# Second attention layer in pairs: two heads to a score bank, two to a transposing bank, copies by ScalarE alone

## What is computed

```python
h = norm(x) * (1.0 + scale) + shift
q = rope(h @ Wq.T)                       # 16 heads
c_kv = h @ Wkd.T                         # latent of 128
k, v = rope(c_kv @ Wku.T), c_kv @ Wvu.T  # 4 heads, each used by 4 query heads
scores = q @ k.T / sqrt(32)              # blocked and windowed: -inf outside
attn = softmax(scores)
x = x + (attn @ v) @ Wo.T
```

## Time and profile before

| | |
|---|---|
| median of 3 runs | 2899.52 us (2898.2 to 2907.24) |
| the profiled execution | 2904.38 us, its span 2902.6 us, mean granted clock 0.894 |
| L1 attention, first load to its last output matmul | 1178.6 to about 1646 us of the span |
| its tile loop | 1224 to 1625 us |
| PE / DVE / ACT / POOL busy in the whole span | 2427.1 / 1624.0 / 1213.8 / 908.3 us |

### The profile page before, as it was taken

The page is one execution under the profiler, slowest core; times in us unless marked ns, Lnnn a source line. Parts: engine busy times, 40 slices in busy tenths (PEclk is TensorE's granted clock), DMA queues, the critical chain, the costliest instruction groups (busy, mean ns, idle before and its releaser), DMA issues. The chain is left out here.

```text
span 2902.6 us, 47820 instructions
## 1 busy us (share of the span) xinstructions
PE 2427.1 (84%) x15668; PEld 1962.4 (68%) x15668; DVE 1624.0 (56%) x4635; ACT 1213.8 (42%) x2990; POOL 908.3 (31%) x982
## 2 busy tenths in 40 slices
PE   4878789798589999688888568889689999996786
PEld 2767677677477888466666457777578888885565
DVE  3777766677654443566556466566543333333876
ACT  2565565566331111366656445556431111112443
POOL 0234332233376676223223113223212112110422
PEclk7989889899899999788678679999899999997898
DMA  6000000000200000100000000000101000001000
GB/s 230 1 1 1 9 2 9 1 2 9 88 15 30 15 29 0 71 30 2 2 1 1 31 4 1 1 0 1 46 20 37 30 22 22 0 0 47 1 29 29
DMA packets 15887, 63.16 MB, mean 22 GB/s; under 512 B 2604, under 2 KB 3500, under 8 KB 10692
## 3 DMA queue, kind: packets, MB, share of 16 engines
q1 hardware_dynamic: 15684, 60.65, 5.8%
HBM read 56.42 MB, written 4.23 MB: 21 GB/s over the span
## 5 line engine op out<-in xcount | busy, mean ns | idle before, releaser
L871 ACT ACTIVATE l0a_prob<-l0a_prob,l0a_nmin 128x512 f32<-128x512 f32 x256 | 185.8, 726 | 202.9 <-DVE l0a_nmin L1129 202.5
L1673 POOL TENSOR_TENSOR l2m_hidl<-l2m_hid,l2m_hidh 128x512 fp32r<-128x512 f32 x64 | 100.9, 1577 | 480.2 <-DVE l2m_hidh L1645 480.2
L1293 POOL TENSOR_TENSOR l0a_prob<-l0a_prob,l0a_rinv 128x512 f32<-128x512 f32 x64 | 66.7, 1042 | 517.9 <-DVE l0a_rinv L1136 517.9
L1529 ACT ACTIVATE l2m_gate<-l2m_psG 128x512 f32<-128x512 f32 x64 | 38.3, 598 | 452.0 <-PE l2m_psU L1462 452.0
L1640 DVE TENSOR_TENSOR l2m_hid<-l2m_gate,l2m_psU 128x512 f32<-128x512 f32 x64 | 44.0, 688 | 300.1 <-ACT l2m_gate L1529 300.1
L702 PE MATMUL l0a_psT<-res_ident,l0a_prob 128*128 128x128 f32 x1024 | 166.2, 287 | 12.0 <-ACT l0a_PT L881 11.8
L1129 DVE CUSTOM_DVE_ANT_0 l0a_prob<-l0a_psS,l0a_mask 128x512 f32<-128x512 f32 x256 | 173.3, 688 | 2.6 <-issue 1.6
L1692 POOL TENSOR_TENSOR res_X<-res_X,l0m_share 128x512 f32<-128x512 f32 x128 | 161.8, 1292 | 25.7 <-DVE l0m_share L1629 24.7
L680 PE MATMUL l0a_psS<-l0a_kT,l0a_qT 96*128 96x512 f32 x256 | 127.9, 501 | 43.5 <-DVE l0a_nmin L1129 28.6
L560 PE MATMUL l0a_psA<-l0a_wh,l0a_hTh 128*128 128x128 f32 (+1 forms) x512 | 152.2, 297 | 12.7 <-DVE l0a_wl L1244 5.8
L702 PEld LDWEIGHTS l0a_psT<-res_ident,l0a_prob 128*128 128x128 f32 x1024 | 133.9, 148 | 38.9 <-ACT l0a_PT L881 17.9
(11 more groups left out here) (399 smaller groups left out, 7785.3 us busy)
## 6 DMA issues: line engine op xcount, KB each, us to landing
l2m_stage<-in_l2m_w SPq DMA_DIRECT2D x8, 1536.0 KB, 6.7
l0m_stage<-in_l0m_w SPq DMA_DIRECT2D x8, 1024.0 KB, 4.8
cond_w<-in_wmod SPq DMA_DIRECT2D x6, 1024.0 KB, 7.9
res_X<-in_x SPq DMA_DIRECT2D x4, 1024.0 KB, 13.4
l0a_prob<-in_l0a_w SPq DMA_DIRECT2D x4, 1024.0 KB, 6.6
l1a_wmod<-in_wmod SPq DMA_DIRECT2D x4, 1024.0 KB, 6.0
out<-res_X SPq DMA_DIRECT2D x4, 1024.0 KB, 4.3
l_stage<-in_l_w SPq DMA_DIRECT2D x3, 1024.0 KB, 7.2
```

The costliest lines, as they stand in the source:

```text
L871: act.activation(prob[:, n % NP, 0:w], src[:, 0:w], ACT.Exp, bias=nmin[:, n % NP:n % NP + 1], scale=-1.0, accum_out=ssum[:, n % NP:n % NP ...
L1293: op = pool.tensor_tensor(x, x, r.to_broadcast([P, w]), ALU.mult)
L1673: pool.tensor_tensor(hidl[:, s % 2, m, :], hid[:, m, :], f32(hidh[:, s % 2, m, :]), ALU.subtract).then_inc(hl_done, 1)
```

## The change

In L1 the tiles go in pairs of heads (2p, 2p + 1):

- `s_bank(n)` is n // 2 mod 3 and `s_part` puts the second head at column 256: a bank of psS holds two tiles. AHEAD is 2: an even step n issues the scores of tiles n + 2 and n + 3, an odd step none. The wait is for the minima of the pair before in that bank, five tiles back; `s_done` rises by two after the second matmul.
- the transposes of both heads go in the odd step n, for tiles n - 7 and n - 6, into the two halves of a psT bank; `pT_mm` rises by two at the end. The wait is for the copy two pairs back.
- ACT copies both heads with one ACTIVATE (128 x 512, or 128 x 256 for the first query tile) in the next, even step, ahead of the exponential. DVE copies none.
- `weigh` waits for the copy of the second pair.
- the plan of jobs is as it was.

Beside this, R.sc and R.cT are kept with 4 columns; the padded array c32 is made where it is used: by ACT in the first stage, and by POOL (`padded_rows`: a memset and two copies) at the start of the L0 MLP and of the L1 attention. `pick` is loaded again in each of these two stages, one more DMA on SP ahead of the weights, and their counts on `small_in` rise by one. The instructions of L0 and L2 attention, of the L2 MLP and of the experts are the same.

```diff
+def padded_rows(pool, R, c32, c32_zero, c32_done):
+
+    pool.memset(c32[:], 0.0).then_inc(c32_zero, 1)
+    pool.wait_ge(c32_zero, 1)
+    pool.tensor_copy(c32[:, 0, :, 0:B], R.sc[:])
+    pool.tensor_copy(c32[:, 1, :, 0:B], R.cT[:]).then_inc(c32_done, 1)
...
-    AHEAD = 2 if L is L0 else 1
+    AHEAD = 1 if L is L2 else 2
...
-        NSMALL = 3 if is1 else 2
+        NSMALL = 4 if is1 else 2
...
             n = n % NTILE
+            if is1:
+                return n // 2 % NS
...
-            return next(d for d in range(1, NTILE) if s_bank(n - d) == s_bank(n))
+            return next(d for d in range(1 + is1, NTILE) if s_bank(n - d) == s_bank(n))
+
+        def s_part(n):
+
+            return n % 2 * 256 if is1 else 0
...
+                    sp.dma_start(pick[:], D["pick"]).then_inc(small_in, 16)
...
-                    if n >= since(n) or not first:
+                    if is1 and n % 2 == 1:
+                        pass
+                    elif n >= since(n) or not first:
                         pe.wait_ge(min_done, b * NTILE + (n - since(n) + 1))
...
+                        if n % 2 == 0:
+                            return
...
-                    mm.then_inc(s_done, 1)
+                    mm.then_inc(s_done, 2 if is1 else 1)
 
                 def pT_copied(b, m):
 
+                    if is1:
+                        return pT_act, 2 * U * b + (m // 2 + 1)
...
                 def transposes(b, m, first):
 
-                    if not (first and m < 2):
-                        pe.wait_ge(*pT_copied(b, m - 2))
+                    if is1 and m % 2 == 0:
+                        return
+                    if not (first and m < 2 + 2 * is1):
+                        pe.wait_ge(*pT_copied(b, m - 2 - 2 * is1))
...
+                    for i in ((m - 1, m) if is1 else (m,)):
...
-                        if n + AHEAD < NTILE:
-                            scores(b, n + AHEAD, first)
-                        elif more and n < NTILE:
-                            scores(b + 1, n + AHEAD - NTILE, False)
+                        for k in ((n + AHEAD, n + AHEAD + 1) if is1 and n % 2 == 0 else () if is1 else (n + AHEAD,)):
+                            if k < NTILE:
+                                scores(b, k, first)
+                            elif more and n < NTILE:
+                                scores(b + 1, k - NTILE, False)
...
+                    if is1:
+                        act.activation(PT[:, j - 1:j + 1, 0:w],
+                                       psT[m // 2 % 2].rearrange("p (j w) -> p j w", j=2)[:, :, 0:w],
+                                       ACT.Copy).then_inc(pT_act, 1)
+                        return
...
-                        copy = m is not None and (m - CL) % 4 < 3 and m - CL < NTILE and not (first and m < CL)
+                        copy = m is not None and m - CL < NTILE and not (first and m < CL)
+                        copy = copy and ((m - CL) % 2 == 1 if is1 else (m - CL) % 4 < 3)
...
-                        if m is not None and (m - CL) % 4 == 3 and m - CL < NTILE and not (first and m < CL):
+                        if not is1 and m is not None and (m - CL) % 4 == 3 and m - CL < NTILE and not (first and m < CL):
```

More of the change, by code:

```diff
@@ L106, in bcast_rows, with modulation_products @@
     return bass.AP(ap.tensor, ap.offset, [[0, n]] + list(ap.ap))
-def modulation_products(pe, R, g, w, ps):
-    src = R.sc if g in MOD_COND else R.cT
+def modulation_products(pe, rows, g, w, ps):
+    src = rows[:, 0 if g in MOD_COND else 1]
     for k in range(NK):
@@ L149, in condition @@
         rows = S.sb("rows", [P, 2, C])
+        pick = S.sb("pick", [P, B])
+        c32 = S.sb("c32", [P, 1, NK, COLS])
+        c32_zero = S.sem("c32_zero")
         pm = [S.ps(f"pm{i}", [P, 512]) for i in range(2)]
@@ L189, in _ @@
                 act.wait_ge(small_in, 8 * 16)
-                act.activation(R.sc[:], R.cT[:], ACT.Silu).then_inc(silu_done, 1)
+                act.activation(R.sc[:], R.cT[:], ACT.Silu)
+                act.wait_ge(c32_zero, 1)
+                act.activation(c32[:, 0, :, 0:B], R.cT[:], ACT.Silu).then_inc(silu_done, 1)
                 act.wait_ge(tabs, 1)
@@ L205, in sums @@
                         pe.wait_ge(mod_read, g - 1)
-                    modulation_sums(pe, R, rows[:, g % 2], ps[g % 2]).then_inc(mod_sum, 1)
+                    modulation_sums(pe, pick, rows[:, g % 2], ps[g % 2]).then_inc(mod_sum, 1)
                 pe.wait_ge(silu_done, 1)
@@ L226, in _ @@
             def _(v):
+                v.memset(c32[:], 0.0).then_inc(c32_zero, 1)
                 v.wait_ge(id_done, 1)
@@ L631, in run @@
                         pe.wait_ge(mod_rows, x + 1)
-                        modulation_sums(pe, R, rows, psA[i]).then_inc(mod_sum, 1)
+                        modulation_sums(pe, pick, rows, psA[i]).then_inc(mod_sum, 1)
                         freed[i] = [(mod_done, x + 1)]
@@ L673, in scores @@
                             pe.wait_ge(kT_done, L.nks * (g + 1))
-                    if n >= since(n) or not first:
+                    if is1 and n % 2 == 1:
+                        pass
+                    elif n >= since(n) or not first:
                         pe.wait_ge(min_done, b * NTILE + (n - since(n) + 1))
                     w = L.width[qt]
-                    q, out = qT[:, j, qt * P:(qt + 1) * P], psS[s_bank(n)][:, 0:w]
+                    q, out = qT[:, j, qt * P:(qt + 1) * P], psS[s_bank(n)][:, s_part(n):s_part(n) + w]
                     if is0:
@@ L694, in transposes @@
                 def transposes(b, m, first):
-                    if not (first and m < 2):
-                        pe.wait_ge(*pT_copied(b, m - 2))
+                    if is1 and m % 2 == 0:
+                        return
+                    if not (first and m < 2 + 2 * is1):
+                        pe.wait_ge(*pT_copied(b, m - 2 - 2 * is1))
                     pe.wait_ge(p_done, b * NTILE + (m + 1))
                     qt = m // 4 % NT
-                    for c in range(L.parts[qt]):
-                        k0 = (FAR if qt and c == 0 else 0) if is1 else c * P
-                        mm = pe.transpose(psT[m % 2][:, c * P:(c + 1) * P], prob[:, m % NP, k0:k0 + P], R.ident[:])
-                    mm.then_inc(pT_mm, 1)
+                    for i in ((m - 1, m) if is1 else (m,)):
+                        ps = psT[m // 2 % 2][:, i % 2 * 256:] if is1 else psT[m % 2]
+                        for c in range(L.parts[qt]):
+                            k0 = (FAR if qt and c == 0 else 0) if is1 else c * P
+                            mm = pe.transpose(ps[:, c * P:(c + 1) * P], prob[:, i % NP, k0:k0 + P], R.ident[:])
+                    mm.then_inc(pT_mm, 2 if is1 else 1)
                 def weigh(b, u, first):
                     hg, qt = divmod(u % U, NT)
-                    pe.wait_ge(*pT_copied(b, 4 * u + 2))
+                    if not is1:
+                        pe.wait_ge(*pT_copied(b, 4 * u + 2))
                     pe.wait_ge(*pT_copied(b, 4 * u + 3))
@@ L1128, in minima @@
                     v.memset(beat[:, n % NP:n % NP + 1], 0.0)
-                    v.tensor_tensor_reduce(prob[:, n % NP, 0:w], psS[s_bank(n)][:, 0:w], other,
+                    v.tensor_tensor_reduce(prob[:, n % NP, 0:w], psS[s_bank(n)][:, s_part(n):s_part(n) + w], other,
                                            -L.scale, BIG, ALU.add, ALU.min,
@@ L1476, in sums @@
                         pe.wait_ge(mod_read, n)
-                    modulation_sums(pe, R, rows, psM[1]).then_inc(mod_sum, 1)
+                    modulation_sums(pe, pick, rows, psM[1]).then_inc(mod_sum, 1)
                 body(0, True)
                 if not swiglu:
+                    pe.wait_ge(c32_done, 1)
                     modulation(0, L1_SCALE)
@@ L2072, in layout @@
     a = {k: np.asarray(v) for k, v in i.items()}
-    d = {"x": a["x"], "condT": np.pad(tiles(a["cond_2048"].T), ((0, 0), (0, 0), (0, COLS - B)))}
+    d = {"x": a["x"], "condT": tiles(a["cond_2048"].T)}
     d["pick"] = np.tile(np.eye(COLS, B, dtype=np.float32), (NK, 1))
```

35 lines of the change are left out of this document (23 added, 12 removed).

## The result

The changed kernel took 2952.35 us in the median of 4 runs (2951.14 to 2959.52), the kernel before 2899.7 us. The ratio is 1.0171, with a 95% interval of 1.0149 to 1.0193: 52.6 us slower, where the forecast was 22.4 us slower and the range ended at 2947.

A forecast was written before the change was run, and what follows sets the result against it. No engine was taken to fill L1's tile loop: PE, DVE and ACT are late in turn, PE waiting 41.4 us. Terms -10 + 1.5 + 0 + 21.6 + 4.8 + 3.6 + 0.9 = +22.4 on 2899.5 gave 2922 us, range 2882 to 2947.

The forecast's parts named there:

- the step it rested on: L1 group boundaries: paired scores, issued sooner, make PE wait for ACT's qT copies; +21.6, +4.8 and +3.6 us.
- the price of a boundary: L1 waits for qT: 2.4 us at nine ordinary boundaries, +4.8 at three with output projections, +3.6 at three with the latent.
- the ring of psT: L1 transposes wait two pairs back, but `weigh` waits for ACT's later copy: +1.5 us for three units, 0 elsewhere.
- The copies: L1 loop: DVE loses 63 copies, 24.5 us of work, counting where DVE sets the pace: -10 us, between 0 and -24.5.
- Pairs on prob and psS: L1 loop: even tiles' minima need transposes one step later, psS has five tiles of slack: 0, between -3 and +3 us.
- Starts: Stage starts in L1 attention and the MLP: one more DMA on SP delays small loads and weights, +0.9 us.
- Rival 2: L1 loop: pausing once a unit, PE stays at 1.2 GHz, 0.8 us a unit, about 2946 us; chance 0.12.
- Rivals 1 and 3: 1: half of the 41.4 us recovered, boundaries free, about 2880 us, chance 0.21. 3: gains and waits cancel, 2900, 0.15.
- Outside L1: L0 and L2 attention, whose loops are unchanged, should keep their times.

The follow-up runs named there:

- q_early: Changed kernel with the next head group's q and k transposes two and one steps earlier, so ACT's qT copies come two steps earlier: L1 attention 482.68 us, ratio 1.0087.
- scores_paired: Changed kernel with L1 transposes, their copies and `weigh` one by one as before; scores still paired, two ahead: L1 attention 508.82 us, ratio 1.0126.
- weigh_last: Changed kernel with `weigh` in L1 moved behind the transposes of its step, not ahead of the scores: L1 attention 489.84 us, ratio 1.0122.
- transposes_paired: Changed kernel with L1 scores one by one, one ahead, three banks as before; transposes and copies still paired on ACT: L1 attention 472.03 us, ratio 1.0048.
- side_only: Changed kernel without any pairs in L1 attention, keeping padded rows, the pick tile and extra DMAs: L1 attention 467.99 us, ratio 1.0012.
- late_slots: Changed kernel with each pair of scores issued one step later and 16 half-width prob slots in place of 8: L1 attention 498.49 us, ratio 1.0111.
- best_without_side: Kernel before plus L1 transposes paired on ACT, 16 prob slots and `weigh` behind transposes, without padded rows or pick tile: L1 attention 459.23 us, ratio 0.9960.

## Why the prediction was right or wrong

- **Direction, and the step it rested on.** Right. PE waits for qT before scores 33.0 us in 39 waits (said: 25 to 35 in 24 to 30), on two units at every boundary, and q_early gives 29.7 us back. The tile loop took 445.1 us, where about 423 was said.
- **The step that failed: the price of a boundary.** 21.6 + 4.8 + 3.6 = 30.0 us was said for scores in pairs, 40.8 measured. By scores_paired the nine ordinary boundaries cost 30.7 us (3.4 each, 2.4 said), the three with the latent 8.9 (3.6 said, on the ground that the first wait lay under another), and the three with output projections 0.7 (4.8 said): there the waits (1.3 us a boundary in the changed kernel) hardly lengthened the units. At the last boundary the two units went from 9.84 to 13.30 us: +3.46, where the text had followed the chain to +3.5 and then taken 2.4, on the ground that PE could give back part of its waits for copies. It gave nothing back there. The full price, at nine boundaries, would have made 31.5 for 21.6; in the changed kernel the nine cost 35.1.
- **The second step that failed: the ring of psT.** The mechanism was named (`weigh` waits for ACT's second copy, the transposes come behind it), and its reach was mis-sized: +1.5 us for three units and 0 elsewhere. (The steps of its sum make 3.48 us, not 3.4, and in the last group the second and third unit went from 2.68 and 3.07 us to 3.82 and 4.18, some 1.1 each for the 0.5 said.) weigh_last shows 22.6 us of it in the changed kernel, 17.8 of them in the loop, and 14.8 with single scores, 9.7 in the loop. The sentence that elsewhere other work fills the gap was wrong. The wait before `weigh` was to be near 15 us or grow; it grew to 41.0.
- **The copies.** Said -10 us. DVE did lose 15.2 us of busy time (24.5 us of copies were counted), and transposes_paired was 4.0 us slower all the same: -8.5 (with the ring's 1.5) was said for this half, so 12.5 us are missing here. The gain is real but was held behind `weigh`: with 16 slots and `weigh` last this half gives -12.3 us against side_only, 8.6 of them in the loop. ACT's copies took what was said:

```profile
L920 ACT ACTIVATE l1a_PT<-l1a_psT 128x512 f32<-128x512 f32 x95 | 56.6, 596 | 50.2 <-PE l1a_psT L738 50.1
...
L920 ACT ACTIVATE l1a_PT<-l1a_psT 128x256 f32<-128x256 f32 x32 | 11.9, 371 | 0.0
```

- **Pairs on prob and psS.** Said 0 (-3 to +3). A wait of 120.6 us stood there, and 16 slots gave 6.1 us: outside the band, though far less than the wait looked like.
- **Starts.** Said +0.9. From the stage's first DMA to the first scores it is 45.4 us before and 45.5 after; nothing is to be seen.
- **Rival 2, the clock.** The loop's clock fell from 0.77 to 0.70, the bound that was named. It is a part of the loss, not what started it. Changes of order alone, q_early and `weigh` last, take the 44 us away, and with them the clock of L1 attention goes back from 0.71 to 0.76. Where the clock was near 1.2 GHz before too, a boundary still costs 2.9 us of the 4.4 that it costs elsewhere. No run held the clock fixed, so the part of it is known only by that estimate, some 9 us at the nine boundaries. **Rivals 1 and 3** were wrong: the full 25.8 us of waits of transposes for copies did go, and PE only waited elsewhere.
- **Outside L1.** 8.6 us of the 52.6, a difference of medians, are not in L1 attention as profiled (by the ratio of 1.0171 it would be some 5.5). The prediction had that L0 and L2 attention keep their times. L2 did, to 0.3 us. L0 attention is the subject of the last section.

In sum: of the 30.2 us that the forecast was short, 22.5 lie in L1 attention. Measured apart they are 10.8 for scores in pairs and 12.5 for the copies and the ring, where `weigh` stood in front (0.8 us more than both together). The other 7.7 lie outside. A cost of the side part of some 5 us, and L0 attention's variation, would fill them; neither is shown.

## What to carry to other kernels

When a change takes a wait off a queue, look for other instructions in the same queue that wait for the same event: here `weigh` waited for the copy that the transposes no longer needed, and moving it behind them was worth 15 to 23 us with pairs (5 of them behind the loop, at a higher clock) and cost 7 without. Issuing work in pairs makes the second one's inputs due a step earlier; move their producers with it, or pair only the side whose inputs are there. A large wait of an engine off the path (120.6 us) says little on what its removal brings (6.1 us): give the engine what it waits for and see what is late next.

## What was not expected of the hardware

L0 attention runs the same 5632 matmuls in every kernel here, written by the same lines, and took from 727 to 748 us by execution. The two kernels without the side part were at 730.55 and 733.56 us, the 18 others at 737.5 in the mean; with one profile of each that isn't enough to tell a cause from chance. Its time goes with the granted clock: 730.55 us at 0.91 in the kernel before, 727.34 at 0.91 in side_only, 740.86 at 0.88 after, and in late_slots:

```profile
37.23:785.36 748.13, 616.91 (x5632) 522.65 (x5632) 510.22 (x1548) 425.25 (x1012) 230.85 (x272) 0.87 0.04 12
```

DVE's busy time in the stage keeps within 2.6 us over all these kernels and ACT's within 1.2; PE's is here 23 us longer than before's. A difference of 10 us in one profile of this stage is thus no sign of a change, while L1 attention repeated within 0.4 us in the two pairs of kernels that have the same code there (only best_without_side, 3.3 us apart, did not), though its clock is lower. What makes the clock of L0 attention differ between executions, no run here shows.
